# Graph attention and a two-expert FFN on one core: a new first stage, and edge rows summed on a PSUM accumulator three slots at a time

## What is computed

```
feat_all = einsum('ni,rhid->rnhd', layernorm(x), conv_weights)      # 8 relations, 4 heads of 64
el = sum(feat_src_e * attn_l[type]);  er = sum(feat_dst_e * attn_r[type])
e  = leaky_relu(el + er);  alpha = softmax of e over the edges of one destination
h  = segment_sum(alpha * feat_src_e, edge_dst) + h_bias;    x = x + h
# FFN on layernorm(x): gate softmax, top 2 of 8
out = sum over e of cw[:, e] * (gelu(xf @ W1[e] + b1[e]) @ W2[e] + b2[e]);   x = x + out
```

## Time and profile before

| | |
|---|---|
| median of 3 runs | 2590.69 us (2589.88 to 2595.78) |
| the profiled execution | 2589.21 us, span 2587.5 us |
| mean granted TensorE clock | 0.772 |
| busy PE / PEld / DVE / ACT / POOL | 1421.4 / 1140.8 / 1207.6 / 646.3 / 1346.7 us |
| first DMA of the second stage | 426.77 us after the span's start |
| last write of the result | issued at 2576.1 us |

### The profile page before, as it was taken

How to read it: one execution, slowest core, us unless ns; L and a number is a source line. 1 busy time by engine, 2 the same in 40 slices (tenths; PEclk the granted TensorE clock), 3 DMA queues, 4 the chain that set the end, 5 groups by cost and what they waited for, 6 DMA issues and landing times.

```text
span 2587.5 us, 26491 instructions
## 1 busy us (share of the span) xinstructions
PE 1421.4 (55%) x7174; PEld 1140.8 (44%) x7174; DVE 1207.6 (47%) x2265; ACT 646.3 (25%) x2349; POOL 1346.7 (52%) x1199
## 2 busy tenths in 40 slices
PE   2738960006625554444655555555666666656687
PEld 1314430005514544444545544445555565555575
DVE  6430023425625553434555554545455555554472
ACT  2213320102202222211222222222323222322241
POOL 2405042868876555566555555556565656565600
PEclk9869985557857886777777777777778787877798
DMA  5724336433332222222222222222222222222300
GB/s 151 196 65 118 131 136 181 136 88 87 84 99 72 62 66 63 74 80 76 68 63 66 62 65 68 70 72 72 72 68 69 72 67 72 70 74 70 73 12 3
DMA packets 113020, 213.04 MB, mean 82 GB/s; under 512 B 58254, under 2 KB 70133, under 8 KB 108838
## 3 DMA queue, kind: packets, MB, share of 16 engines
q0 software_dynamic: 57264, 152.04, 22.1%
q1 hardware_dynamic: 38688, 25.68, 3.8%
q10 hardware_dynamic: 16892, 33.82, 3.5%
HBM read 170.97 MB, written 44.87 MB: 83 GB/s over the span
## 4 chain that ended last, share of the span: by engine, by line
another core or an unknown queue 28%; issue 20%; PE 18%; DVE 10%; ACT 7%; DVEq 1%; ACTq 0%; POOL 0%; POOLq 0%
PE hid_ps L1422 10%; PE y_ps L1436 6%; ACT hT L1332 4%; ACT rows L1342 2%; DVE score L980 1%; DVE er_hot L978 1%; DVE xo L1177 1%; DVE rows L1025 1%; PE gate_ps L1414 1%; DVE rows L1020 1%; PE zt_ps L1446 1%; DVE hot L976 0%; DVE xo L1169 0%; ACT zT L1320 0%
## 5 line engine op out<-in xcount | busy, mean ns | idle before, releaser
L873 POOL DMA_INDIRECT rows<-table,idx_st x1008 | 1145.0, 1136 | 509.1 <-issue 308.6
L1436 PE MATMUL y_ps<-w,hT 128*128 128x256 f32 (+1 forms) x1920 | 512.4, 420 | 395.6 <-ACT hT L1332 241.4
L1436 PEld LDWEIGHTS y_ps<-w,hT 128*128 128x128 f32 (+1 forms) x1920 | 381.8, 207 | 487.1 <-ACT hT L1332 271.3
L1422 PE MATMUL hid_ps<-zT,w 128*128 128x128 f32 (+1 forms) x3840 | 521.0, 299 | 0.5 <-issue 0.5
L1422 PEld LDWEIGHTS hid_ps<-zT,w 128*128 128x128 f32 x3840 | 508.5, 215 | 17.4 <-ACT hT L1332 9.6
L1177 DVE SCALAR_TENSOR_TENSOR xo<-y_ps,cw,xo 128x256 f32<-128x256 f32 (+1 forms) x240 | 115.7, 482 | 703.2 <-remote 645.2
L1332 ACT ACTIVATE hT<-hid_ps,b1t 128x128 f32<-128x128 f32 (+1 forms) x960 | 271.5, 367 | 640.2 <-PE hid_ps L1422 301.6
L1025 DVE TENSOR_TENSOR rows<-rows 128x2080 f32<-128x2080 f32 x106 | 246.2, 2323 | 39.8 <-ACT rows L1342 31.3
L586 PE MATMUL feat_ps<-wc,xnT 128*125 128x512 f32 x480 | 232.2, 629 | 52.7 <-ACT xnT L519 36.2
L1020 DVE TENSOR_TENSOR rows<-rows,ex 128x2080 f32<-128x2080 f32 (+1 forms) x136 | 256.2, 1903 | 1.7 <-DVE rows L1020 0.2
L1414 PE MATMUL gate_ps<-gw,zT 128*128 128x8 f32 x120 | 29.9, 359 | 383.1 <-ACT zT L1320 382.6
(11 more groups left out here) (172 smaller groups left out, 973.5 us busy)
## 6 DMA issues: line engine op xcount, KB each, us to landing
table<-stage ACTq DMA_DIRECT2D x30, 1031.2 KB
rows<-table,idx_st POOLq DMA_INDIRECT x1008
w<-in_L_ffn_W_dram SPq DMA_DIRECT2D x16, 512.0 KB
blocks<-edge_row SPq DMA_DIRECT2D x1, 4351.5 KB, 62.3
x_all<-in_x_dram SPq DMA_DIRECT2D x3, 1250.0 KB
node_tab<-x_all SPq DMA_DIRECT2D x3, 1250.0 KB
wc<-_L_gnn_conv_weights_dram ACTq DMA_DIRECT2D x16, 128.0 KB, 6.7
attnb<-in_L_gnn_attn_l_dram SPq DMA_DIRECT2D x1, 1024.0 KB, 11.9
```

Of the source, the lines that this page charges most:

```text
L873: q.indirect_dma_start(buf[:, k, :], None, table, bass.IndirectOffsetOnAxis(idx[:, col + k:col + k + 1], 0)).then_inc(landed, 16)
L1422: last = t.matmul(hid_ps[e % 2][:, m * P:m * P + n], w1[:, e, k, m * P:(m + 1) * P], zT[:, k, 0:n], start=(k == 0), stop=(k == KD - 1))
L1436: last = t.matmul(y_ps[p % 2][0:n, (e % 2) * D:(e % 2 + 1) * D], hT[e % 2][:, k, 0:n], w2[:, e, k, :], start=(k == 0), stop=(k == KH - 1))
```

## The change

The function `shift_steps` goes. In the **first stage**:

- `conv_weights` come re-laid by the host as [128, 2, 2048] and are loaded with 2 DMAs instead of 16. The attention vectors are loaded as one row and spread to 128 partitions by PE (K = 1 matmuls) and ACT; the same is done for the firsts of the 198-edge blocks, instead of a way through DRAM.
- Every load or store of 125 partitions becomes two, of 112 and 13 partitions (`spread`). `stage` has 4 buffers (before 2), `xnT` 4 (2); a tile's scores come 2 tiles later (`LAG`). PE's and ACT's code for the 30 tiles is written out instead of looped.
- `start` is sought for 31 node positions a partition, so that `deg` is a difference within a partition, with no DRAM between. `rank_w`, `nb_d` are replaced by PE transposes; `ranked` is laid out by partition; `blocks` goes: each node's list is fetched from `edge_row` at its true start (`idx_all`, u32).
- `node_tab` is stored in three parts as the tiles get ready.

In the **second stage**: `ex` is written a second time, to PSUM; `er9` lies in PSUM; slots 0 to 2 are weighed straight into three PSUM lanes; the other slots are weighed in place and added to the lanes three slots at a time (780 columns); the three lanes are then summed into `acc`. ACT weighs slots 21 to 31 (11, before 7). `sums` and its 8 identity matmuls go. Groups are fetched in the order 0 to 3, each on `freed`. A chunk beyond 64 edges is fetched directly.

```diff
+def spread(rows):
+    return [(lo, hi) for lo, hi in ((0, rows - rows % 16), (rows - rows % 16, rows)) if hi > lo]
...
-            for r in range(R):
-                for k in range(KD):
-                    act.dma_start(wc[:, k, r * D:(r + 1) * D].rearrange("p (h d) -> p h d", h=H),
-                                  conv[r, :, k * P:(k + 1) * P, :].rearrange("h p d -> p h d")).then_inc(conv_in, 16)
+            for k in range(KD):
+                act.dma_start(wc[:, k, :], conv[:, k, :]).then_inc(conv_in, 16)
...
+                for lo, hi in parts:
+                    act.dma_start(table_v[i][lo:hi, :], stage[i % NSTG][lo:hi].rearrange("p r c -> p (r c)")
+                                  ).then_inc(stored[i % NSTG], 16)
...
+            for i in range(T + LAG):
+                if i < T:
+                    products(i)
+                if i >= LAG:
+                    node_scores(i - LAG)
+                if i == AT_OFFS:
...
+            for w in range(W):
+                g.indirect_dma_start(idx_all[:, w, :], None, edge_row.rearrange("(n o) -> n o", o=1),
+                                     bass.IndirectOffsetOnAxis(rank_sb[:, w, 1:2].bitcast(U32), 0)
...
-            for n, s in enumerate((1, 3, 2, 0)):
+            for s in range(PAIRED):
                 if not isinstance(w, int) or w >= 2:
-                    if s:
-                        pool.wait_ge(folded, (w - 2) * 3 + (n + 1))
-                    else:
-                        pool.wait_ge(agg_ok, w - 1)
+                    pool.wait_ge(freed, (w - 2) * PAIRED + (s + 1))
...
             st.did(v.tensor_scalar(ex[:], rden[:], 2.0, -1.0, ALU.mult, ALU.add))
+            st.did(v.tensor_scalar(ex_ps, rden[:], 2.0, -1.0, ALU.mult, ALU.add))
...
+        def weighted(par, lo, hi, out=None):
             r = rows[par][:, lo:hi, 0:AGG].rearrange("p k (h c) -> p k h c", h=H)
+            o = r if out is None else out.rearrange("p k (h c) -> p k h c", h=H)
+            return v.tensor_tensor(o, r, bc(ex_ps[:, :, lo:hi].rearrange("p h k -> p k h"), 3, HC), ALU.mult)
+        def add(par, lo, n=LANES):
+            return v.tensor_tensor(lanes[:, 0:n], rows[par][:, lo:lo + n, 0:AGG], lanes[:, 0:n], ALU.add)
 
         def weigh_all(w, par, st, gate, between):
-            st.did(weighted(par, 0))
+            st.did(weighted(par, 0, LANES, lanes))
+            st.did(weighted(par, LANES, 12))
             for _ in range(2):
                 next(gate, None)
-            st.did(weighted(par, 1))
+            st.did(weighted(par, 12, ACT_LO))
             for _ in range(3):
                 next(gate, None)
             with dve.If(degree > PAIRED * SLOTS):
-                weighted(par, PAIRED)
+                weighted(par, PAIRED * SLOTS, NS)
                 dve.drain()
-                fold(par, 0, PAIRED)
-                dve.drain()
-            fold(par, 0, 1).then_inc(folded, 1)
+                for lo, n in ((32, 3), (35, 3), (38, 2)):
+                    add(par, lo, n)
+                    dve.drain()
+            for lo in (3, 6):
+                st.did(add(par, lo))
+                st.wait()
+            dve.sem_inc(freed, 1)
             for _ in gate:
                 pass
-            st.did(weighted(par, 2))
-            st.did(weighted(par, 3, BY_ACT))
-            st.wait()
+            for lo in (9, 12, 15):
+                st.did(add(par, lo))
+                st.wait()
+            dve.sem_inc(freed, 1)
+            st.did(add(par, 18))
+            between()
             dve.wait_ge(act_weighed, w + 1)
-            fold(par, 2, 3).then_inc(folded, 1)
-            between()
-            dve.wait_ge(folded, w * 3 + 2)
-            fold(par, 0, 2).then_inc(folded, 1)
+            st.did(add(par, 21))
+            dve.sem_inc(freed, 1)
+            for lo in (24, 27):
+                st.did(add(par, lo))
+            st.did(add(par, 30, 2))
+            dve.sem_inc(freed, 1)
+            st.did(v.tensor_copy(acc_f, lanes[:, 0]))
+            st.did(v.tensor_tensor(acc_f, acc_f, lanes[:, 1], ALU.add))
+            v.tensor_tensor(acc_f, acc_f, lanes[:, 2], ALU.add).then_inc(acc_ok, 1)
...
-            sums(w, par)
```

More of the change, by code:

```diff
@@ L198, in phase1 @@
         hb = t("hb", [TN, D])
-        stage = [t(f"stage{i}", [TN, R, ROW]) for i in range(2)]
+        stage = [t(f"stage{i}", [TN, R, ROW]) for i in range(NSTG)]
         er_all = t("er_all", [TN, T, RH])
@@ L594, in node_scores @@
                 for k in range(KD):
-                    last = m.matmul(score_ps[0:TN, 0:2 * RH], xnT[par][:, k, :], wa[:, k, :], start=(k == 0),
+                    last = m.matmul(score_ps[0:TN, 0:2 * RH], xnT[i % NXT][:, k, :], wa[:, k, :], start=(k == 0),
                                     stop=(k == KD - 1))
                 last.then_inc(score_ok, 1)
-            def tiles(lo, hi):
-                with pe.Fori(lo, hi) as pair:
-                    for par in range(2):
-                        products(pair * 2 + par, par)
-                        node_scores(pair * 2 + par, par)
@@ L662, in phase2 @@
     typ_cur = [sb(f"typ_cur{i}", [P, CHUNK]) for i in range(2)]
-    er9 = [sb(f"er9{i}", [P, H, R1]) for i in range(2)]
     hot9 = sb("hot9", [P, NS, R1])
@@ L864, in _ @@
         q = nc.gpsimd
-        for i in range(2):
-            q.memset(er9[i][:], MASKED).then_inc(const_ok, 1)
         bt = Batches(pool, "pool")
@@ L1267, in _ @@
         dve.sem_inc(cleared, 1)
+        for i in range(2):
+            v.memset(er9[i], MASKED).then_inc(const_ok, 1)
         dve.wait_ge(const_ok, 2)
@@ L1446, in b2_term @@
             t.matmul(b2_ps, cwT[:], b2s[:], start=True, stop=True).then_inc(b2_ok, 1)
-        def sums(w, par):
-            pe.wait_ge(folded, w * 3 + 3)
-            for k in range(SLOTS):
-                last = t.matmul(agg_ps[:, 0:AGG], ident[:], rows[par][:, k, 0:AGG], start=(k == 0),
-                                stop=(k == SLOTS - 1))
-            last.then_inc(agg_ok, 1)
         def window(w, par, half):
```

587 lines of the change are left out of this document (295 added, 292 removed).

## The result

| | before | changed |
|---|---|---|
| median, us | 2591.86 (2589.88 to 2595.78) | 2644.91 (2643.26 to 2645.69) |
| ratio, 95% interval | | 1.0202 (1.0184 to 1.0220) |
| first DMA of the second stage, us | 426.8 | 307.7 |
| mean of 24 looped windows, us | 68.1 | 73.8 |
| mean burst of 34 / 28 gathers, us | 47.5 / 41.3 | 42.4 / 34.9 |

The change made the kernel 2% slower. Of the later executions of the kernel before, one took 2849 us beside six of 2228 to 2241 us; it is a slow one and enters no ratio. The first stage gained 119 us. The second lost 175: 23 in the first five windows, 137 in the 24 looped ones (5.7 each), 15 behind the last `node_row`.

The account below looks back on a forecast made before the run. No engine is full, so waits decide: a looped window is a ring of `zT` to first release, POOL's burst, and 5 us to the next `zT`. 2589.2 - 146 - 70 = 2373, so 2375 us as run median; range 2290 to 2560.

Parts of the forecast that it names:

- First stage, -146: First stage: split stores, extra buffers and earlier PE start bring the second stage's first DMA from 426.8 to 281 us.
- My bound of 320: First stage: latest expected time, in us, of the second stage's first DMA, with POOL's bursts at their upper bound.
- two more buffers take off most of the waits for `stage`: First stage: two extra buffers alone remove most of ACT's 120.1 us, as stores exceed PE by 0.7 us a tile.
- The first release, +2.3 us a window: Looped windows over 32 slots: DVE's first weighing to first release of `rows` grows from 12.7 to 15.0 us.
- The burst, -4.8 us a window: Second stage: POOL's gathers, no longer slowed beside DVE's two-SBUF-operand work, take 4.8 us less a window.
- The rule on the shared port: Second stage: two-SBUF-input DVE operations lock a port pair GpSimd shares; one PSUM operand avoids it, removing the gathers' excess.
- The last piece, taken as 5 us as before: Looped window, end of POOL's burst to the next `zT`: stays 5 us.
- what PE finishes during the burst comes late anyway: Second stage: the reason for costing PE's loss of 8 identity sums at nothing.
- PE is late beyond the burst: Rival, looped windows: leftover PE work adds 4.5 us behind the burst, +126, 2500 us; 0.29 shared with two other cases.
- Slower: Rival, looped windows: PE gets nothing through during back-to-back gathers, +12 us a window, +336, 2709 us; chance 0.08.
- 34.9 us of work in nearly 63 us: Second stage, argument against late PE: a whole window's work of 34.9 us has nearly 63 us to pass in.
- The lag goes: Rival, second stage: PE's lateness vanishes and POOL alone sets 48 to 50 us windows, 1950 to 2000 us; chance 0.09.

Follow-up runs that it names:

- e11: Kernel with new first stage and old sum, each 125-partition transfer in one piece again, four `stage` buffers kept; 0.988 of the kernel before, in a set without hold-up.
- e5: Changed kernel with the lanes, the second copy of `ex` and `er9` in SBUF instead of PSUM; 0.960 of the kernel before.
- e13: The changed kernel itself run again, in a set without the hold-up; 1867.56 us against 2238.66 for the kernel before, ratio 0.835.
- e18: Changed kernel with lanes, `ex` and `er9` in SBUF, run again in a set without the hold-up; 0.896 of the kernel before.
- e1: New first stage with the old second stage (but for the fetch beyond 64 edges); 2453.99 us against 2566.48 for the kernel before, ratio 0.956.
- e4: Changed kernel gathering half rows, 528 bytes instead of 1056, same number of gathers; 2632.65 us where the kernel before took 2566.
- e6: Changed kernel with one small POOL memset, waiting for the one before, behind each of a window's 28 fixed gathers; 0.989 of the kernel before.
- e7: Changed kernel with POOL also waiting, before group 2 (slots 16 on), until DVE has written `z`; 1.130 of the kernel before.
- e8: Kernel with new first stage and old sum, POOL waiting for `z` before the third group it fetches; 0.907 of the kernel before.
- e2: Changed kernel with a POOL drain after each gather of rows; 1.706 of the kernel before.

## Why the prediction was wrong

I forecast 2375 us (2290 to 2560) and faster with 0.90. Measured: 2645.

- **First stage, -146: right in kind, -119 in size.** PE's 7.52 us a tile, ACT's missing waits, and no DRAM on the edge chain are all there. The thirty tiles took 245.7 us with what the bursts cost (the 24.47 us from 236.95 to 261.42 above all), where I had 247. What I missed is the two ends. The first product stood at 40.79, not 28: PE waited 12.48 us for ACT's `xn`. And from the last product, at 286.5, to the second stage it took 21.2 us, not 6: the last scores ended at 289, and stores of `table` and `node_tab` went one after another on ACT and SP until 304. My bound of 320 held it. That two more buffers take off most of the waits for `stage` was wrong: e11 has them, and ACT waits 133.1 us.
- **The first release, +2.3 us a window: right in kind, +1.0 in size.** Windows must be compared with their like, for two kinds take turns. In the kind of the earlier trace rows `zT` to the first gather grew from 20.5 to 22.1 us, in the other from 18.0 to 19.0. From first weighing to first release it took 14.3 us in both (with over 32 slots), where I had 15.0; before, it was 12.7 in the one, from which I took my price, and 13.3 in the other. ACT and POOL in a window of the first kind:

```profile
1386.28 0.37 ACT L1334 COPY zT<-zt_ps 128x256 f32<-128x256 f32 x1 [5.68 <-PE zt_ps L1424]
```

```profile
1408.34 0.95 POOL L878 DMA_INDIRECT rows<-table,idx_st  x1 [14.05 <-DVEq L1052]
```

- **The burst, -4.8 us a window: right, -5.7 in the mean.** 42.4 for 34 and 34.9 for 28, the plain 1.25 us that I worked out; all gathers near 0.95. The rule on the shared port (the Trainium skill, "SBUF — State Buffer", "SBUF: two separate sides") agrees, for the gathers, with e5 and with e13 to e18.
- **The last piece, taken as 5 us as before, and with it "what PE finishes during the burst comes late anyway", costed at nothing: this is the step that failed.** The piece went to 15.2 us in the mean. The 5 us are what it takes until the hold-up ends, and they stayed (5.6). They were the whole piece only because PE had made the transposes before the burst ended; I took that as given, and the change took it away: 9.6 us of PE's and DVE's work now stand behind the hold-up. Over 24 windows the +10.6 us are some 254 us, against 119 of the first stage and 113 of the first release and the burst; the first five windows and the end lose 38 more.
- **The weighing of the rivals.** "PE is late beyond the burst" named what happened, a part of PE's work left over, but priced it at 4.5 us. "Slower", at 0.08, had the size, +12 us a window, but for PE getting nothing through; most of its work does get through. Against the first I set 34.9 us of work in nearly 63 us. That counts time, not the state that the time is in. The earlier trace rows already showed that nothing of PE's reaches ACT from some point of a burst on; the question was how much work stands before that point. In the window of the earlier trace rows the kernel before has distances of up to 2.9 us at the start of the burst and an unbroken 1.25 us only from 1481.35 on, 12.9 us behind the first gather; the changed kernel has it from the first gather.
- **"The lag goes", 0.09 at 1950 to 2000 us:** it is what happens without the hold-up, where the changed kernel takes 1868 (before 2239). I tied it to the change; it belongs to the condition of the run.

Shown by runs are the place of the operands (e5 against the changed kernel), the other half of the change (e1), that bytes have no part (e4), and that gaps in a burst cut the hold-up short (e6). That the stretched gathers at the start of the burst are what saves e5, by moving its unbroken part later, is read from its trace and not tested by itself. What the hold-up is inside the chip, and why it is in three sets and not in the other three, is not settled: no run here controls it. Late instruction fetch is a rival that no run tests; the traces don't speak for it, since the DMA queue for instructions moved two packets (0.02 MB) between 1482 and 1540 us in the changed kernel, and six between 997 and 1045 us in e13, where nothing is held up.

## What to carry to other kernels

Before a faster producer is credited with its saved time, list what the other engines still have to do when its burst starts, and where in the burst they were seen to stop. A lock that slows a burst can be what lets the others work: try the change with the old operand place as a control, and a small pause within the burst, whose effect depends on what it then runs into (e7 lost 13%, e8 gained 9%, both against the kernel before). Take the verdict from more than one set of runs: the same program took 2% more and 16% less time than its predecessor.

## What the runs showed of the hardware

- While POOL issues indirect gathers at 1.25 us, the other engines can come to a state in which DVE issues one instruction in 1.4 us and PE a matmul in 2.8 us, and ACT waits up to 36 us for PE's semaphore (28 us behind PE's matmul in the window shown), until 3 to 7 us behind the last gather. It sets in 5 to 20 us into the burst. Half the bytes change nothing (e4); gaps of 2.0 to 2.8 us in the burst end it early (e6); at 3.5 us a gather it is not seen (e2). In other sets it is absent at 1.25 us (e13).
- A `drain` on POOL behind a gather costs 2.3 us a gather (e2: 3.5 us from gather to gather in place of 1.25).
- Gathers beside DVE operations with two SBUF operands are stretched, by a mean of 0.35 us a gather when most of DVE's work reads so (1297 against 946 ns); DVE's own time doesn't change (970 against 973 ns).
- With stores of 125 partitions in one piece ACT waited 133 us in 30 tiles with four buffers, and one issue on SP took 40 us; with 112 and 13 partitions ACT waited 2.9 us.
